# A recurrent layer's gate order, cell path and output rows rearranged in a five-stage graph kernel

## The reference, cut to the last layer

```python
x_proj = jnp.einsum('btd,gd->btg', x, W_ih) + b_ih + b_hh
def step(carry, xp):
    h, c = carry
    gates = xp + h @ W_hh.T
    i, f, g, o = jnp.split(gates, 4, axis=-1)
    c = sigmoid(f) * c + sigmoid(i) * jnp.tanh(g)
    h = sigmoid(o) * jnp.tanh(c)
    return ((h, c), h)
```

## Time and profile before

| | us |
|---|---|
| median of 3 runs | 4451.14 |
| range of the runs | 4450.52 to 4453.53 |
| span of the profiled execution | 4442.7 |
| recurrent layer, steps | about 2930 to 4366 of the span |
| busy over the span | PE 3984.7, DVE 3491.9, ACT 2883.5, POOL 1183.3 |

### The profile page before, as it was taken

How to read it: one execution, slowest core, us unless ns; L and a number is a source line. 1 busy time by engine, 2 the same in 40 slices (tenths; PEclk the granted TensorE clock), 3 DMA queues, 4 the chain that set the end, 5 groups by cost and what they waited for, 6 DMA issues and landing times. The chain is left out here.

```text
span 4442.7 us, 143559 instructions
## 1 busy us (share of the span) xinstructions
PE 3984.7 (90%) x55713; PEld 2856.6 (64%) x55713; DVE 3491.9 (79%) x9562; ACT 2883.5 (65%) x7050; POOL 1183.3 (27%) x1032
## 2 busy tenths in 40 slices
PE   7999999996999999999997999978888888888882
PEld 5666666653665666666665777767777777777772
DVE  6999999985889889888986888846666666666666
ACT  6999999985888888888884777733333333333330
POOL 4777877762222222222221101100000000000000
PEclk9999999998999999999998999999999999999996
DMA  2222221210000000000002433411111111111115
GB/s 66 79 81 68 77 76 59 77 58 32 30 20 30 29 25 25 30 29 20 29 20 85 149 127 130 137 41 33 43 36 44 35 42 37 42 36 43 37 40 162
DMA packets 327039, 251.03 MB, mean 57 GB/s; under 512 B 172889, under 2 KB 291033, under 8 KB 324313
## 3 DMA queue, kind: packets, MB, share of 16 engines
q1 hardware_dynamic: 324824, 233.40, 18.1%
q10 hardware_dynamic: 1536, 8.39, 0.5%
HBM read 157.27 MB, written 67.12 MB: 51 GB/s over the span
## 5 line engine op out<-in xcount | busy, mean ns | idle before, releaser
L2578 PE MATMUL lstm_G_psum<-next_Whh,lstm_HT 128*32 128x192 f32 x8192 | 439.8, 332 | 254.9 <-DVE lstm_HT L2710 254.9
L2649 ACT ACTIVATE lstm_TC<-lstm_G_psum 128x192 f32<-128x192 f32 x512 | 169.9, 332 | 690.7 <-PE lstm_G_psum L2578 690.7
L1565 ACT ACTIVATE ssm_EX<-ssm_Z_psum,ssm_tok 128x256 f32<-128x256 f32 (+1 forms) x1024 | 372.6, 424 | 155.2 <-PE ssm_Z_psum L1396 85.5
L2578 PEld LDWEIGHTS lstm_G_psum<-next_Whh,lstm_HT 128*32 128x32 f32 x8192 | 213.9, 109 | 340.3 <-DVE lstm_HT L2710 306.8
L2570 PE MATMUL lstm_G_psum<-next_Wih,lstm_XT 128*32 128x192 f32 x8192 | 427.7, 327 | 0.0
L2697 DVE SCALAR_TENSOR_TENSOR lstm_AB<-lstm_TC 128x128 f32<-128x128 f32 x512 | 149.6, 292 | 290.2 <-ACT lstm_TC L2649 289.0
L616 ACT ACTIVATE g_PR<-g_S,g_nmax 128x512 f32<-128x512 f32 x512 | 368.4, 723 | 4.0 <-DVE g_nmax L751 4.0
L758 DVE COPY g_PT<-g_PT_psum 128x512 f32<-128x512 f32 x512 | 344.4, 684 | 24.0 <-PE g_PT_psum L485 19.3
L607 ACT ACTIVATE g_relu<-g_Z_psum,g_src 128x512 f32<-128x512 f32 x512 | 347.0, 685 | 17.5 <-PE g_Z_psum L478 17.4
L2872 POOL TENSOR_SCALAR lstm_rstd<-lstm_mv 128x4 f32<-128x4 f32 x32 | 7.2, 226 | 1310.0 <-DVE lstm_mv L2691 1310.0
L751 DVE CUSTOM_DVE_ANT_0 g_S<-g_Z_psum,g_relu 128x512 f32<-128x512 f32 x512 | 345.4, 684 | 8.4 <-ACT g_relu L607 6.9
(11 more groups left out here) (307 smaller groups left out, 10906.8 us busy)
## 6 DMA issues: line engine op xcount, KB each, us to landing
g_ADJ<-in_adj SPq DMA_DIRECT2D x64, 1024.0 KB, 7.2
x<-g_XO SPq DMA_DIRECT2D x64, 512.0 KB, 5.3
g_X<-in_x SPq DMA_DIRECT2D x32, 512.0 KB, 4.3
ssm_X<-x SPq DMA_DIRECT2D x32, 512.0 KB, 3.8
x<-ssm_OUT SPq DMA_DIRECT2D x32, 512.0 KB, 2.8
g_X<-x SPq DMA_DIRECT2D x32, 512.0 KB, 4.3
lstm_U<-x SPq DMA_DIRECT2D x128, 128.0 KB, 3.4
lstm_V<-lstm_U SPq DMA_DIRECT2D x128, 128.0 KB, 3.3
```

The lines of the kernel that those rows point to most:

```text
L1565: ins = act.activation(EX[h % NE][:, col:col + n], Zb[c][:, i * CHUNK:i * CHUNK + n], ACT.Exp, bias=tok[b.slot][:, i, c, h:h + 1])
L2578: ins = pe.matmul(bank[32 * j:32 * (j + 1), 0:last - first], HT[t % 2][:, 32 * kc:32 * (kc + 1)], Whh[:, kc, j, first:last], start=False, ...
```

## The change

Five things are changed, all in `lstm_phase`.

1. **Gates.** There are three groups of gates instead of two: f alone, then i and g together, then o. Each is matmulled, tanh'ed and released on its own: f in a bank of its own (Fb), i and g in the first 128 columns of G, o in Ob. Fb and Ob have one buffer each instead of two. Per step TensorE issues 48 + 48 + 12 + 4 instructions instead of 32 + 32 + 8 + 4.
2. **Cell.** AB becomes two operations of 64 elements: KP = (TF + 1) * C as soon as f is there, and IN = (i + 1) * g. The new cell 0.5 * KP + IN is written twice: to columns 128 to 191 of bank G, from where ACT takes its tanh, and right behind it to C in SBUF.
3. **Waits.** H waits for tc first and TO second in the code, so that the wait for tc is the one that rides on the instruction.
4. **Output rows.** The ten 512-element operations go to POOL, for all chunks but the last: the two `own` at the start of the following chunk, ahead of `scales`, and two series of four behind it. Each operation of a series waits for the one before it; a series begins when DVE's running sums have come far enough (nine, then seventeen). The sums are spread anew: one in each of steps 3 to 6 and two in each of steps 8 to 13.
5. ACT normalises after steps 9 and 10 instead of 8 and 9.

Core of the diff:

```diff
-        Ob = [m.ps(f"O{k}") for k in range(2)]
+        Fb = m.ps("F")
+        Ob = m.ps("O")
...
             def hidden(c, t):
-                for bank, first, last, made in ((Gb[t % 2], 0, IFG, s["g"]), (Ob[t % 2], IFG, 4 * HB, s["go"])):
+                for gate, made in (("f", s["gf"]), ("ig", s["g"]), ("o", s["go"])):
...
             def gates(c, t):
+                c.wait(act, s["gf"], S, t + 1)
+                c.wait(act, s["keep"], S, t)
+                act.activation(TF[:, :], Fb[:, 0:HB], ACT.Tanh).then_inc(s["tf"], 1)
                 c.wait(act, s["g"], S, t + 1)
-                c.wait(act, s["ab"], S, t - 1)
-                act.activation(TC[t % 2][:, 0:3, :].rearrange("p g e -> p (g e)"), Gb[t % 2][:, 0:IFG], ACT.Tanh
+                c.wait(act, s["inp"], S, t)
+                act.activation(IG[:, :, :].rearrange("p g e -> p (g e)"), Gb[t % 2][:, 0:2 * HB], ACT.Tanh
...
             def cell(c, t):
-                act.activation(tc[:, :], TC[(t + 1) % 2][:, 3, :], ACT.Tanh, scale=0.5).then_inc(s["tc"], 1)
+                act.activation(tc[:, :], Gb[t % 2][:, 2 * HB:3 * HB], ACT.Tanh, scale=0.5).then_inc(s["tc"], 1)
...
             def step(c, t):
+                c.wait(v, s["tf"], S, t + 1)
+                c.wait(v, s["c2s"], S, t)
+                v.scalar_tensor_tensor(out=KP[:, :], in0=TF[:, :], scalar=1.0, in1=C[:, :], op0=ALU.add, op1=ALU.mult
+                                       ).then_inc(s["keep"], 1)
                 c.wait(v, s["tg"], S, t + 1)
-                c.wait(v, s["c2"], S, t)
-                v.scalar_tensor_tensor(out=AB[:, :, :], in0=TC[t % 2][:, 0:2, :], scalar=1.0, in1=TC[t % 2][:, 2:4, :],
-                                       op0=ALU.add, op1=ALU.mult).then_inc(s["ab"], 1)
-                c.wait(v, s["ab"], S, t + 1)
-                v.scalar_tensor_tensor(out=TC[(t + 1) % 2][:, 3, :], in0=AB[:, 1, :], scalar=0.5, in1=AB[:, 0, :],
+                v.scalar_tensor_tensor(out=IN[:, :], in0=IG[:, 0, :], scalar=1.0, in1=IG[:, 1, :], op0=ALU.add,
+                                       op1=ALU.mult).then_inc(s["inp"], 1)
+                c.wait(v, s["inp"], S, t + 1)
+                c.wait(v, s["keep"], S, t + 1)
+                v.scalar_tensor_tensor(out=Gb[t % 2][:, 2 * HB:3 * HB], in0=KP[:, :], scalar=0.5, in1=IN[:, :],
                                        op0=ALU.mult, op1=ALU.add).then_inc(s["c2"], 1)
+                v.scalar_tensor_tensor(out=C[:, :], in0=KP[:, :], scalar=0.5, in1=IN[:, :],
+                                       op0=ALU.mult, op1=ALU.add).then_inc(s["c2s"], 1)
+                c.wait(v, s["tc"], S, t + 1)
                 c.wait(v, s["to"], S, t + 1)
-                c.wait(v, s["tc"], S, t + 1)
...
             def body(c):
-                if c.reg is not None or c.off < CH - 1:
+                if c.off > 0:
+                    for hf in range(2):
+                        own(g, c + -1, hf)
+                if c.off < CH - 1:
                     scales(c + 1)
+                if c.off > 0:
+                    for hf in range(2):
+                        before_it(g, c + -1, hf)
+                        before_added(g, c + -1, hf)
+                        up_to_it(g, c + -1, hf)
+                        up_to_taken(g, c + -1, hf)
```

More of the change, by code:

```diff
@@ L2444, in lstm_phase @@
     HALF = S // 2
-    IFG = 3 * HB
     with ExitStack() as ctx:
@@ L2519, in move @@
             def move(c):
-                c.wait(sp, s["done"], 1, 1)
+                c.wait(sp, s["u"], 6, 6)
                 q, r = c.index() // PER, S * (c.index() % PER)
@@ L2560, in inputs @@
                     c.wait(pe, s["xt"], KC, KC)
-                for bank, first, last, read in ((Gb[t % 2], 0, IFG, s["tg"]), (Ob[t % 2], IFG, 4 * HB, s["to"])):
-                    c.wait(pe, read, S, t - 1)
-                    n = last - first
+                for gate in ("f", "ig", "o"):
+                    if gate == "f":
+                        c.wait(pe, s["tf"], S, t)
+                    if gate == "ig":
+                        c.wait(pe, s["tg"], S, t - 1)
+                    if gate == "o":
+                        c.wait(pe, s["to"], S, t)
                     for j in range(J):
-                        pe.matmul(bank[32 * j:32 * (j + 1), 0:n], ones_bf[:, :],
-                                  bias[:, 4 * HB * j + first:4 * HB * j + last],
+                        pe.matmul(into(gate, t, j), ones_bf[:, :], of_gate(bias[:, 4 * HB * j:4 * HB * (j + 1)], gate),
                                   start=True, stop=False, skip_group_check=True)
@@ L2569, in inputs @@
                         for j in range(J):
[L2570 to L2571 removed]
+                            pe.matmul(into(gate, t, j), XT[c.slot][:, kc, :, t], of_gate(Wih[:, kc, j, :], gate),
+                                      start=False, stop=False, skip_group_check=True)
             def hidden(c, t):
[L2574 removed]
+                for gate, made in (("f", s["gf"]), ("ig", s["g"]), ("o", s["go"])):
                     for kc in range(KC):
@@ L2577, in hidden @@
                         for j in range(J):
-                            ins = pe.matmul(bank[32 * j:32 * (j + 1), 0:last - first],
-                                            HT[t % 2][:, 32 * kc:32 * (kc + 1)], Whh[:, kc, j, first:last],
-                                            start=False, stop=(kc == KC - 1), skip_group_check=True)
+                            ins = pe.matmul(into(gate, t, j), HT[t % 2][:, 32 * kc:32 * (kc + 1)],
+                                            of_gate(Whh[:, kc, j, :], gate), start=False, stop=(kc == KC - 1),
+                                            skip_group_check=True)
                     ins.then_inc(made, 1)
@@ L2722, in gate_out @@
                 c.wait(v, s["repp"], 1, 1)
+                c.wait(v, s["part"], 4, 0)
                 v.tensor_copy(gS[:, :], LGb[c.slot][:, REP_AT:REP_AT + S]).then_inc(s["gs"], 1)
```

132 lines of the change are left out of this document (59 added, 73 removed).

## The result

| | before | changed |
|---|---|---|
| median, us | 4451.65 | 4788.37 |
| range, us (4 runs each) | 4450.52 to 4453.53 | 4781.58 to 4798.12 |
| span of the profiled execution | 4442.7 | 4779.7 |
| one chunk of 16 steps (mean of chunks 2 to 30) | 44.42 | 55.09 |

The changed kernel is slower by 337 us: ratio 1.0757, with a 95% interval of 1.0743 to 1.0772. The forecast was 4531 with 4450 to 4620 as its range. The sign was right; the loss was over four times as large as forecast (337 against 80) and lies outside the range.

What follows compares the result with a forecast made beforehand. The prediction took the ring of dependent operations, not any full engine, as the bound: 4442.7 - 113 (shorter step) - 5 (later normalising) + 198 (POOL's rows) + 8.4 outside the span = 4531 us, range 4450 to 4620.

Steps and rivals of the forecast that it cites:

- the shorter path: Recurrent step falls from 2.76 to 2.54 us, gaining 113 us over 512 steps, plus 5 us for normalising one step later.
- POOL's rows holding DVE: Large output-row operations on POOL block DVE's two-SBUF-input operations: 6.4 us a chunk, +198 us over 31 chunks (183 to 245).
- TensorE's total: TensorE works 2.19 us a step, bias matmuls add about 0.03, and 36 more instructions don't count; the 2.54 step holds that.
- the ring: Dependency chain from one start of the hidden matmuls to the next; it sets the step, 2.76 us before, 2.54 forecast.
- Rival 3: POOL blocks at its high end and DVE's PSUM write or TensorE's weight loads add 0.1 a step: 4629 us; chance 0.12.
- The waits: Swapping H's two waits cuts the gap between tc's end and H from 0.10 to 0.03 us: -0.07 a step.
- The PSUM cell: New cell written to PSUM and read there by ACT: -0.037 a step; DVE's PSUM write taken at 0 extra.
- Normalising later: The step that waited for POOL's shift took 2.93 instead of 2.76; normalising one step later gains 5 us over 31 chunks.
- my low end: POOL's rows cost a chunk 5.9 us if DVE operations that don't wait for each other hold together.
- Rival 1: POOL's output rows cost nothing, so only the path's gain shows: 4333 us; chance 0.12.
- rival 2: POOL blocks DVE, but less than counted, 3 to 4.5 us a chunk: 4426 to 4472 us; chance 0.08.
- The high case of POOL: POOL also gets in between DVE operations that don't wait for each other: 3.5 us a series, 7.9 us a chunk.

Runs made afterwards that it cites:

- kept busy: Changed kernel without the input projection of f and o, plus three 448-column matmuls on TensorE in steps 10 and 14, rows on POOL: 4523.99 us.
- 80 loads, rows on DVE: Changed kernel with output rows and running sums back on DVE and the input projection of f and o left out: 4347.32 us.
- 80 loads: Changed kernel, output rows on POOL, with the input projection of f and o left out (80 weight loads a step instead of 112): 4560.13 us.
- 112 loads: Weight loads a step, each with a matmul, in the whole changed kernel, rows on POOL: 4788.37 us; with its rows on DVE: 4742.25 us.
- the swap: Kernel before with only the two waits of H swapped: 4430.37 us, ratio 0.9952.
- with TensorE kept busy: Whole changed kernel, nothing left out, plus three 448-column matmuls on TensorE behind the logit matmuls of steps 10 and 14: 4801.57 us.
- the three parts that add none to TensorE: Kernel before with H's waits swapped, new cell written to bank G and then SBUF, and normalising one step later: 4394.49 us, ratio 0.9874.

## Why the prediction was right or wrong

**Where the 337 us are.** Two pairs of kernels and the one kept busy give the parts, each as a difference of medians:

| part | us | forecast |
|---|---|---|
| the shorter path (80 loads, rows on DVE, against before) | -104 | -118 |
| POOL's rows holding DVE (80 loads, kept busy, against rows on DVE) | +177 | +198 |
| TensorE's clock after the stalls (80 loads, against kept busy) | +36 | 0 |
| TensorE's instruction supply (112 loads against 80) | +228 | 0 |

The split depends on the order in which the parts are added: the supply alone, with the rows on DVE, costs 395 (4742.25 - 4347.32), since it then has no stalls of DVE to hide in.

1. **The step that failed is "TensorE's total"**: "36 more instructions don't count each: 16 matmuls with their loads of 64 columns pass in 0.22, 0.014 each". It took the time of a pair within a block for the rate at which pairs can be had, and so put the supply of instructions at nothing. At 112 loads the ring of 2.54 would need a block in 128 x 2.54 / 112 = 2.90 us; one takes 3.8. It cost 228 us, more than twice the way from the forecast to the top of its range (89). The supply gives 93 loads per 2.76 us. The kernel before, with 76, lay under that, so no row of it could show the limit as a wait; its queue row (449 packets for 7.36 MB, one in 4.64 us in the steps) shows only the ring's own rate. It could have told me that the change asks for blocks faster than any steps in the trace had had them; I didn't ask.
2. **Rival 3 named the right resource and refused it** by the same 0.014. It would have put 0.1 a step on the path. The supply put 228 / 512 = 0.45, or 0.77 with the rows on DVE.
3. **The shorter path was right.** The step is 2.554 for 2.54. The waits gave 0.072 (forecast 0.07). The PSUM cell gave 0.024 (2.688 to 2.664) for 0.037; by the means of that kernel tc took 0.223 (I had 0.219) and DVE's write to PSUM 0.233 instead of 0.226, a term that I had taken at 0 within bounds of 0 to 0.04. The two make up 0.011 of the missing 0.013.
4. **Normalising later** was forecast at 5 us, on the 0.17 by which that step was long. It is worth more beside a shorter step, where DVE's row holds POOL's shift: without it the swap gives back 17 us.
5. **POOL's rows holding DVE were right in kind and a little high.** Without the clock a chunk pays 46.82 - 41.10 = 5.7 us, against 5.9 at my low end and 6.4 taken. By place: 0.87 at the start (forecast 0.9), 2.40 for a series (2.43), 0.17 in step 11 (0.1). I went above the low end in case POOL slips in between KP and IN; it didn't.
6. **The clock was left out.** I read 1.00 in the earlier trace rows and carried it over to a kernel in which TensorE stands idle for 3.2 us at a time. It costs 36 us with 80 loads. In the changed kernel itself steps 11 and 15 were 0.44 and 0.25 longer than with TensorE kept busy, 21 us over 31 chunks, but that run gave it back in steps 10 and 14.
7. **The 8.4 us outside the span** were not fixed. Where a run has both numbers, the time is 1.7 to 2.4 us above the span. So the profiled execution before was probably one of the faster ones, and my sum carries the difference on; it is a few us and decides nothing.

Rival 1 is out by the rows of over 1 us on DVE, and rival 2 (3 to 4.5 us a chunk) by the 5.7. The high case of POOL (7.9) is out too; the 7.0 measured with 80 loads is 5.7 and the clock.

**Left open** is how the supply works inside: how many blocks are held, what starts a fetch, and how much of the 3.8 comes from the other transfers. In the changed kernel a packet mostly begins 1.13 us after a pause ends and the next pause ends 2.3 to 2.6 us after it begins, which sum to about 3.5 to 3.8. That would fit a fetch that starts only when the block before it has been entered, but nothing was run that could tell.

## What to carry to other kernels

Count the instructions of an unrolled loop per turn, not only their columns: on TensorE here a load and a matmul cost 0.030 us of supply though they pass in 0.014, and the limit shows as nothing until it is crossed, then as pauses "<-issue" in the middle of ready work. An edit that splits an instruction to shorten a chain must pay for all its copies; of this change the three parts that add none to TensorE gave 1.3%, and 36 added pairs alone cost 281 us, more than the whole shorter path gains (104). Moving work to an engine whose large operations hold up those of the first can put a wait onto the path, and the idle time can cost a second time through TensorE's clock.
